# A wait of POOL for p, filler products at set-up and seam, late statistics moved behind the seam, W a on DVE

## The chip, the core and the metric

The kernel runs on one core of a Trainium2 chip. The core has a matrix engine (PE), a vector engine (DVE), an activation engine (ACT), a general engine (POOL) and a queue that issues transfers (SP); each works through its own instructions in order and waits on semaphores for the others. The metric is the device time in microseconds from start to end of one execution; the median of three runs is given.

## The reference

There are 128 graphs of 128 nodes with 256 features. Two residual layers follow each other:

```
n  = layernorm(x);  Wh = n @ W
e  = leaky(Wh@a1 [i] + Wh@a2 [j], 0.2) + log(adj + 1e-6)
x1 = x + softmax_j(e) @ Wh
m  = layernorm(x1)
w  = softmax(mean_graphs(m) @ Wr + br)              # per node, 8 experts
h  = relu(bn1(m @ W1[e] + b1));  h = relu(bn2(h @ W2[e] + b2))
out = x1 + sum_e w[node, e] * (h @ Wo[e] + bo[e])
```

So the gate w of a node needs the normalised x1 of all graphs, and no output can be formed before the last graph has gone through the first layer.

## The kernel before, in words

Four graphs are a group; there are G = 32 groups. The program has two blocks with a barrier between them, here called the seam: the graph stage and the expert stage.

**Graph stage.** Every engine runs `step(g, layer)` for g = -1 to 33, software-pipelined by hand: in step g, PE projects group g, scores and p are formed for a = g - 1, the product with p and x1 for b = g - 2, and the sum of normalised x1 over graphs (`acc`, in the tile resb) for h = g - 4. x1 of even groups lies in the tile h2, x1 of odd groups in w_bc. Steps 6 to 21 are a loop of 8 pairs (layer = 1, here the first loop), in which W1's seven Strassen combinations are prepared, one expert a pair; steps 22 to 29 are a loop of 4 pairs (layer = 2, the second loop) which splits W2 into a high and a low part, one expert a step.

DVE in a step: accumulator adds for two graphs (`add_part`, L608), l_sb (leaky scores, L621), the reciprocal, neg_m (L628), x1 (L646), four p with row sums (L658), statistics of the next x (`stats_1`, L574) and of x1 (`stats_2`, L582). POOL in a step: in the first loop four small sums into w_stage (even step, L451 to L458) or wq_lo (odd step, L463); in the second loop w_lo (L468); then the accumulator add of the other two graphs (L476); then `deviations` (L404 to L424), which turns statistics into dev, the reciprocal standard deviations, for the next x and for an x1. ACT in a step: s_sb (L506), the scaled x1 for POOL (L514), the high parts of weights, e_sb (L526), wh scaled by dev (L541), copies of pT (L557) and xnT (L562). PE in a step: the product p h (L733), the projection (L716), transposes of p (L753), of the next x (L685) and of the scores' column (L762). SP loads x, res and adj, stores x1, and in the first loop waits for wq_lo ahead of the next W1.

At set-up W is centred (its column mean, by a product with the constant tile mean_w, L694, is taken off, L587), then transposed, and W a1 and W a2 are formed on PE and copied into two further columns of the tile gw by way of ACT (L701 to L708, L493 to L496). Then the first projection starts. In the last steps DVE normalises the first tile for the experts (`tile_normalise`, L124) and splits it (`tile_low`, L162), and POOL forms its Strassen sums (`tile_sums`).

**Expert stage.** A unit is one expert of one tile of four graphs; a step handles the first layer of unit n (Strassen products, `strassen`, L1155), the second layer of unit n - 1 (`product`, L171) and the third of unit n - 3 (L1174). DVE's z for the second half of a unit (`sum_2`, L1042) has to be there before the last first-layer product of that unit. At its start DVE takes the statistics of the last group (L1029 to L1033), POOL their deviations (L918 to L925), and DVE adds group 30 to acc (`add_group`, L179); `feature_mean` in step 1 adds group 31 and forms the mean. POOL also forms the low parts of Wo there (L929). SP stores each tile's output when its last half is done (L905).

What orders the work around the change is written out by hand; there is no planner.

## Time and profile before

| | us |
|---|---|
| median of three runs | 2380.46 |
| lowest, highest | 2379.27, 2383.46 |
| the profiled execution | 2380.82 |
| its span, first to last instruction | 2379.0 |

| engine | busy us of the span | share |
|---|---|---|
| PE | 2339.6 | 98% |
| DVE | 1687.8 | 71% |
| ACT | 1615.7 | 68% |
| POOL | 435.0 | 18% |

The shares are means over both stages. The mean granted clock of PE over the span is 0.994; it has two levels, 1.2 and 2.4 GHz, and 1.00 is the upper one. A row of a window is its start and end, its length, each engine's busy time with its number of instructions, the clock, the share in which the DMA engines were busy, and their rate. A line such as L658 is line 658 of the kernel; a helper's line stands for all its callers. In a timeline, `x4` merges four instructions, and what stands in brackets is the idle time of the engine just before and what ended it.

### The profile page before, as it was taken

To read this page: it belongs to the slowest core of one execution; us is meant where nothing else is said; L and a number is where in the kernel's file an instruction comes from. 1 tells how busy PE (TensorE), PEld (TensorE's weight loads), DVE (VectorE), ACT (ScalarE), POOL (GpSimd) and SP (SyncE) were. 2 spreads that over 40 slices of the span, in tenths; PEclk is the share of its full clock that TensorE was granted. 3 is DMA by queue.
4 is the path that set the end of the run, shared out by engine and by line. 5 is a ranking of instruction groups with operands and counts; after the bars stand their busy time and mean duration, and the time that the engine had idled before them with its cause. 6 is when DMAs were issued, how large, how long until landed. Compare 5 with 4: busy or idle time off the path is not lost.

```text
span 2379.0 us, 46022 instructions
## 1 busy us (share of the span) xinstructions
PE 2339.6 (98%) x16164; PEld 2166.8 (91%) x16164; DVE 1687.8 (71%) x2577; ACT 1615.7 (68%) x2524; POOL 435.0 (18%) x566
## 2 busy tenths in 40 slices
PE   8999799999999999999999999999999999999999
PEld 7777689999999999999999999999999999999998
DVE  5999866666776766676666676666666666677666
ACT  5888676666666666666666666666666666666665
POOL 4898621111101011111111101011111111001010
PEclk9999799999999999999999999999999999999999
DMA  5778410000000000000000000000000000000000
GB/s 175 255 251 267 154 36 27 27 26 26 26 26 25 19 9 26 26 26 26 26 26 26 26 26 18 20 14 26 26 26 26 26 26 26 26 26 18 18 10 27
DMA packets 91178, 116.16 MB, mean 49 GB/s; under 512 B 4700, under 2 KB 78856, under 8 KB 91144
## 3 DMA queue, kind: packets, MB, share of 16 engines
q1 hardware_dynamic: 91144, 115.73, 14.8%
q8 instruction: 19, 0.31, 0.1%
q14 instruction: 15, 0.12, 0.0%
HBM read 82.16 MB, written 33.55 MB: 49 GB/s over the span
## 4 chain that ended last, share of the span: by engine, by line
PE 88%; DVE 0%; ACT 0%; issue 0%
PE ps_y L1174 31%; PE ps_wide L171 30%; PE ps_wide L1155 26%; PE ps_t L132 1%; DVE h_lo L1059 0%; DVE z L1052 0%; ACT h_hi L954 0%; ACT v L959 0%; DVE resb L1082 0%; DVE h_lo L1065 0%; DVE z L1042 0%; PE ps_t L1219 0%; PE ps_t L1201 0%; PE ps_t L1206 0%; ACT featT L985 0%
## 5 line engine op out<-in xcount | busy, mean ns | idle before, releaser
L959 ACT ACTIVATE v<-ps_wide,bn_cols 128x256 f32<-128x256 f32 x768 | 434.1, 565 | 375.0 <-PE ps_wide L1155 245.1
L967 ACT ACTIVATE h<-ps_wide,bn_cols 128x512 f32<-128x512 f32 x512 | 399.2, 780 | 314.2 <-PE ps_wide L171 312.0
L1174 PE MATMUL ps_y<-wo_hi,h_hi 128*128 128x256 f32 x2048 | 579.3, 283 | 0.5 <-DVE h_lo L1065 0.5
L1174 PE MATMUL ps_y<-wo_lo,h_hi 128*128 128x256 f32 x2048 | 579.6, 283 | 0.0
L1174 PE MATMUL ps_y<-wo_hi,h_lo 128*128 128x256 f32 x2048 | 579.5, 283 | 0.0
L1059 DVE SCALAR_TENSOR_TENSOR h_lo<-z,h_hi 128x1024 fp32r<-128x1024 f32 x256 | 313.8, 1226 | 341.6 <-ACT h_hi L954 341.6
L1155 PE MATMUL ps_wide<-xq_hi,wq_hi 128*128 128x256 f32 x1792 | 500.9, 279 | 7.4 <-PEq L185 3.1
L1155 PE MATMUL ps_wide<-xq_lo,wq_hi 128*128 128x256 f32 x1792 | 497.8, 278 | 0.0
L1155 PE MATMUL ps_wide<-xq_hi,wq_lo 128*128 128x256 f32 x1792 | 497.0, 277 | 0.0
L171 PE MATMUL ps_wide<-h_hi,w_lo 128*128 128x512 f32 x1024 | 403.9, 394 | 0.0
L171 PE MATMUL ps_wide<-h_lo,w_hi 128*128 128x512 f32 x1024 | 402.0, 393 | 0.0
L171 PE MATMUL ps_wide<-h_hi,w_hi 128*128 128x512 f32 x1024 | 398.3, 389 | 0.5 <-DVE h_lo L1059 0.5
L1174 PEld LDWEIGHTS ps_y<-wo_hi,h_lo 128*128 128x128 f32 x2048 | 392.5, 192 | 0.0
L1174 PEld LDWEIGHTS ps_y<-wo_hi,h_hi 128*128 128x128 f32 x2048 | 390.4, 191 | 1.1 <-DVE h_lo L1065 0.7
L1174 PEld LDWEIGHTS ps_y<-wo_lo,h_hi 128*128 128x128 f32 x2048 | 390.6, 191 | 0.0
L1065 DVE TENSOR_TENSOR h_lo<-h,h_hi 128x1024 fp32r<-128x1024 f32 x256 | 313.5, 1225 | 85.3 <-ACT h_hi L973 82.1
L938 POOL TENSOR_TENSOR resb<-resb,w_bc 128x512 f32<-128x512 f32 x64 | 85.4, 1336 | 1543.4 <-DMA resb<-x_scratch 1537.4
L1155 PEld LDWEIGHTS ps_wide<-xq_hi,wq_hi 128*128 128x128 f32 x1792 | 340.1, 190 | 19.0 <-issue 3.8
L1155 PEld LDWEIGHTS ps_wide<-xq_hi,wq_lo 128*128 128x128 f32 x1792 | 338.4, 189 | 9.8
L1155 PEld LDWEIGHTS ps_wide<-xq_lo,wq_hi 128*128 128x128 f32 x1792 | 338.2, 189 | 0.0
L1082 DVE SCALAR_TENSOR_TENSOR resb<-ps_y,w_node,resb 128x512 f32<-128x512 f32 x448 | 333.3, 744 | 3.9 <-PE ps_y L1174 3.9
L1052 DVE SCALAR_TENSOR_TENSOR z<-ps_wide,bn_cols,v 128x512 f32<-128x512 f32 x256 | 191.9, 750 | 153.4 <-PE ps_wide L1155 145.9
(131 smaller groups left out, 2995.6 us busy)
## 6 DMA issues: line engine op xcount, KB each, us to landing
x_sb<-in_x SPq DMA_DIRECT2D x32, 512.0 KB, 4.0
res<-in_x SPq DMA_DIRECT2D x32, 512.0 KB, 5.9
x1t<-x_scratch SPq DMA_DIRECT2D x32, 512.0 KB, 3.2
resb<-x_scratch SPq DMA_DIRECT2D x32, 512.0 KB, 3.2
out<-resb SPq DMA_DIRECT2D x32, 512.0 KB, 2.9
adj_sb<-in_adj SPq DMA_DIRECT2D x32, 256.0 KB, 6.1
x_scratch<-h SPq DMA_DIRECT2D x16, 512.0 KB, 4.7
x_scratch<-w_bc SPq DMA_DIRECT2D x16, 512.0 KB, 4.9
```

The lines of the kernel that those rows point to most:

```text
L132: last = nc.tensor.transpose(ps_x[:, c, b4 * N:(b4 + 1) * N], x1t[:, b4, c * P:(c + 1) * P], ident[:, :])
L171: mm = nc.tensor.matmul(acc_ps, w[:, i, c, cols], s[:, c, :], start=start and n == 0, stop=stop and n == len(terms) - 1)
L938: nc.gpsimd.tensor_tensor(resb[:, g, :], resb[:, g, :], ysum[:, g, :], ALU.add).then_inc(resb_done, 1)
L959: nc.scalar.activation(v[:, slot, :], ps_l1[:, 0, 0:H], ACT.Identity, bias=bn_cols[:, 1, cols], scale=bn_cols[:, 0, cols]).then_inc(done, 1)
L967: nc.scalar.activation(h2[:, m, :], ps_l2[:, m, :], ACT.Relu, bias=bn_cols[:, 3, cols], scale=bn_cols[:, 2, cols]).then_inc(r2_done, 1)
L1052: nc.vector.scalar_tensor_tensor(out=z[:, 0, :], in0=ps_l1[:, 1, :], scalar=bn_cols[:, 0, C * e:C * e + 1], in1=v[:, 0:2, :].rearrange("p ...
L1059: nc.vector.scalar_tensor_tensor(out=h1_lo[:, :, :], in0=z[:, :, :], scalar=0.0, in1=h1_hi[:, :, :].bitcast(F32), op0=ALU.max, op1=ALU.sub ...
L1065: nc.vector.tensor_tensor(h2_lo[u[1] % 2][:, :, :], h2[:, :, :], h2_hi[u[1] % 2][:, :, :].bitcast(F32), ALU.subtract).then_inc(lo2_done, 1)
L1082: nc.vector.scalar_tensor_tensor(out=dst[:, g, :], in0=ps_y[:, g, :], scalar=w_node[:, e:e + 1], in1=old, op0=ALU.mult, op1=ALU.add).then_ ...
L1155: mm = nc.tensor.matmul(out_ps, w[:, e, q, :], x[:, q, :], start=start and n == 0, stop=stop and n == len(terms) - 1, skip_group_check=True)
L1174: mm = nc.tensor.matmul(ps_y[:, b4, :], h[:, c, cols], w[:, e, c, :], start=(k == 0 and b4 % per_bank == 0), stop=(k == len(terms) - 1 and ...
```

## The change

- POOL waits in every step of the graph stage for both halves of p of group g - 1 before its first op.
- The statistics of group 0 are taken ahead of the steps; those of x1 of groups 30 and 31 behind the seam, for both together, with their deviations on POOL; both `add_group` calls now stand in `feature_mean`, and ACT waits for the first of them ahead of its first write to h2.
- At set-up a is loaded broadcast to all partitions, DVE forms W a1 and W a2 as four products with row sums ahead of the centring, and PE and a small DVE op centre the two columns. The transposes, ACT copies and small products are gone.
- PE runs filler products whose results nobody reads: seven on mean_w at set-up, five and four in the last two steps of the graph stage, six in each of units 0, 1 and 2 and twelve in unit 0.
- An Exp on ACT stands ahead of everything else of ACT.
- `tile_normalise` of the first tile stands behind p instead of ahead of x1; the third `tile_low` behind the last x1.
- The last tile's output is stored in two halves.

```diff
 # POOL, graph stage
                 def step(g, layer):
+                    a = ago(g, 1)
+                    if exists(a):
+                        pool.wait_ge(p_done, 2 * num(a) + 2)
                     if layer == 1 and g[1] == 0:
...
-                    if exists(nxt) or is_step(g, G - 1) or is_step(g, G):
+                    if exists(nxt) or is_step(g, G - 1):
                         deviations(nxt)
 # ACT, graph stage
+                act.wait_ge(mean_w_set, 1)
+                nc.scalar.activation(neg_m[:, :], mean_w[:, 0:GB], ACT.Exp)
 # DVE, graph stage
+                for b4 in range(GB):
+                    stats_1((0, 0), b4)
+                dve.wait_ge(proj_loaded, 2 * 16)
+                for c in range(C):
+                    for k in range(2):
+                        last = nc.vector.scalar_tensor_tensor(
+                            out=x1t[:, 2 * c + k, :], in0=gw[:, c, 0:D], scalar=1.0, in1=a_bc[:, k, :], op0=ALU.mult,
+                            op1=ALU.mult, accum_out=gw[:, c, D + k:D + k + 1])
+                last.then_inc(va_ready, 1)
...
+                dve.wait_ge(va_mean_ready, 1)
+                nc.vector.scalar_tensor_tensor(out=gw[:, :, D:D + 2], in0=gw[:, :, D:D + 2], scalar=2.0,
+                                               in1=ps_wide[:, 1:2, 0:2].to_broadcast([P, C, 2]), op0=ALU.mult,
...
-                    with_stats = exists(b) and not is_step(b, G - 1)
+                    with_stats = exists(b) and not is_step(b, G - 2) and not is_step(b, G - 1)
...
                     if is_step(g, G):
-                        for group in range(3):
-                            tile_low(dve, 0, group)
+                        tile_low(dve, 0, 0)
+                        tile_low(dve, 0, 1)
+                    if is_step(g, G + 1):
+                        tile_low(dve, 0, 2)
 # PE, graph stage
+                pe.wait_ge(mean_w_set, 1)
+                for _ in range(7):
+                    nc.tensor.matmul(ps_wide[:, 3, 0:P], mean_w[:, :], mean_w[:, :], start=True, stop=True)
                 pe.wait_ge(setup_done, 1)
                 next_rows((0, 0))
...
+                pe.wait_ge(va_ready, 1)
                 for c in range(C):
+                    last = nc.tensor.matmul(ps_wide[:, 1, 0:2], mean_w[:, :], gw[:, c, D:D + 2], start=(c == 0),
+                                            stop=(c == C - 1))
+                last.then_inc(va_mean_ready, 1)
+
+                def keep_clock(n):
+
+                    for _ in range(n):
+                        nc.tensor.matmul(ps_wide[:, 0, 0:D], ident[:, :], gw[:, 0, 0:D], start=True, stop=True)
...
+                    if is_step(g, G + 1):
+                        keep_clock(4)
...
+                    if is_step(g, G):
+                        pe.wait_ge(wh_copied, G)
+                        keep_clock(5)
 # expert stage: SP, POOL, ACT, DVE, PE
+                    if isinstance(t, int) and t == G - 1:
+                        sp.wait_ge(y_done, 2 * E * G - 1)
+                        sp.dma_start(out_g[t, :, 0:HB, :], resb[:, 0:HB, :]).then_inc(out_stored, 16)
+                        sp.wait_ge(y_done, 2 * E * G)
+                        sp.dma_start(out_g[t, :, HB:GB, :], resb[:, HB:GB, :]).then_inc(out_stored, 16)
...
+                pool.wait_ge(last_bnst, 1)
+                nc.gpsimd.tensor_tensor(last_dif[:, :, :], last_st[:, :, :, 1], last_st[:, :, :, 4],
+                                        ALU.subtract).then_inc(last_step, 1)
...
+                        if starts(prev, 0):
+                            act.wait_ge(acc_done, 1)
                         relu_2(prev, 0)
...
-                for b4 in range(GB):
-                    last = nc.vector.bn_stats(last_st[:, b4, :], x1[(G - 1) % 2][:, b4, :])
+                for i in range(2):
+                    for b4 in range(GB):
+                        last = nc.vector.bn_stats(last_st[:, i, b4, :], x1[(G - 2 + i) % 2][:, b4, :])
                 last.then_inc(last_bnst, 1)
...
-                add_group(G - 2)
...
                 def feature_mean():
+                    dve.wait_ge(last_rstd_done, 1)
+                    add_group(G - 2)
                     dve.wait_ge(acc_done, 1)
-                    dve.wait_ge(last_rstd_done, 1)
                     add_group(G - 1)
...
+                def keep_clock(n):
+
+                    for _ in range(n):
+                        nc.tensor.matmul(ps_y[:, 0, :], wq_hi[:, 0, 0, :], xq_hi[:, 0, :], start=True, stop=True)
...
+                    if starts(new, 0) or starts(new, 1) or starts(new, 2):
+                        keep_clock(6)
                     if exists_unit(new):
                         pe.wait_ge(v2_done, uno(new) + 1)
...
+                    if starts(new, 0):
+                        keep_clock(12)
                     if exists_unit(new):
                         pe.wait_ge(z2_done, uno(new) + 1)
```

## Rows read from the trace of the kernel before

**Rows 1.** Windows by stage: PE, PEld, DVE, ACT, POOL busy, clock, DMA, GB/s.

```profile
63.00:188.00 125.00, 118.85 (x642) 99.24 (x641) 122.63 (x402) 106.34 (x280) 112.18 (x185) 1.00 0.77 251
188.00:252.00 64.00, 59.02 (x321) 49.85 (x321) 61.71 (x201) 53.66 (x144) 50.62 (x78) 1.00 0.85 276
...
280.30:297.50 17.20, 14.20 (x51) 12.18 (x52) 11.37 (x25) 7.07 (x12) 4.93 (x7) 0.53 0.35 113
297.50:2376.00 2078.50, 2075.05 (x14799) 1946.30 (x14797) 1428.64 (x1752) 1395.19 (x1948) 215.20 (x194) 1.00 0.07 24
2376.00:2379.00 3.00, 0.00 (x0) 0.00 (x0) 0.00 (x0) 0.00 (x0) 0.00 (x0) 0.94 0.51 175
```

**Rows 2.** Timeline of DVE (start us, us, engine line op): neg_m, one a group.

```profile
62.98 0.69 DVE L628 TENSOR_REDUCE neg_m<-l_sb 128x4 f32<-128x512 f32 x1
...
187.88 0.69 DVE L628 TENSOR_REDUCE neg_m<-l_sb 128x4 f32<-128x512 f32 x1
...
251.89 0.69 DVE L628 TENSOR_REDUCE neg_m<-l_sb 128x4 f32<-128x512 f32 x1
...
269.11 0.69 DVE L628 TENSOR_REDUCE neg_m<-l_sb 128x4 f32<-128x512 f32 x1
```

**Rows 3.** Timeline, first loop, an even step.

```profile
127.81 0.54 DVE L658 SCALAR_TENSOR_TENSOR p_sb<-adj_sb,e_sb 128x128 f32<-128x128 f32 x1
...
131.58 0.85 DVE L608 SCALAR_TENSOR_TENSOR resb<-w_bc,dev,resb 128x256 f32<-128x256 f32 x2
```

**Rows 4.** Timeline, first loop, the odd step ahead of it.

```profile
118.72 1.65 POOL L424 TENSOR_TENSOR dev<-ve,minus_half 128x8 f32 x1 [0.19 <-POOL ve L420]
...
119.84 0.29 DVE L658 SCALAR_TENSOR_TENSOR p_sb<-adj_sb,e_sb 128x128 f32<-128x128 f32 x1
...
120.33 2.17 POOL L463 TENSOR_TENSOR wq_lo<-w_stage,wq_hi 128x896 f32 x1
...
122.47 1.26 POOL L476 TENSOR_TENSOR resb<-resb,x1s_high 128x512 f32<-128x512 f32 x1
...
123.10 1.31 DVE L608 SCALAR_TENSOR_TENSOR resb<-h,dev,resb 128x256 f32<-128x256 f32 x2
...
124.70 0.69 DVE L621 SCALAR_TENSOR_TENSOR l_sb<-s_sb 128x512 f32<-128x512 f32 x1 [0.29 <-ACT s_sb L506]
```

**Rows 5.** Timelines of POOL and DVE, second loop.

```profile
214.13 1.29 POOL L468 TENSOR_TENSOR w_lo<-w_stage,w_hi 128x512 f32 x1 [0.70 <-ACT w_hi L532]
...
214.22 1.35 DVE L658 SCALAR_TENSOR_TENSOR p_sb<-adj_sb,e_sb 128x128 f32<-128x128 f32 x1
```

**Rows 6.** Timeline, set-up, and one projection of the first loop.

```profile
8.05 0.69 DVE L587 SCALAR_TENSOR_TENSOR gw<-gw,ps_wide 128x512 f32<-128x512 f32 x1 [8.05 <-PE ps_wide L694]
...
12.99 5.52 PE L716 MATMUL ps_wide<-gw,xnT 128*128 128x258 f32 x16 [0.26 <-ACT gw L496]
...
124.94 3.65 PE L716 MATMUL ps_wide<-gw,xnT 128*128 128x258 f32 x16
```

**Rows 7.** Timelines of PE, DVE and POOL around the seam.

```profile
271.95 0.77 PE L753 MATMUL ps_pT<-ident,p_sb 128*128 128x128 f32 x4 [2.82 <-DVE p_sb L658]
...
273.47 2.89 DVE L162 TENSOR_TENSOR xq_lo<-xs,xq_hi 128x256 fp32r<-128x256 f32 x3
...
278.72 1.26 POOL L476 TENSOR_TENSOR resb<-resb,x1s_high 128x512 f32<-128x512 f32 x1
...
280.35 1.41 DVE L1029 BATCH_NORM_STATS2 last_st<-w_bc 128x6 f32<-128x256 f32 x4 [1.35 <-PEq L185]
```

**Rows 8.** Timelines, first units of the expert stage.

```profile
280.90 0.41 PE L1155 MATMUL ps_wide<-xq_lo,wq_hi 128*128 128x256 f32 x1
...
286.93 2.50 POOL L929 TENSOR_TENSOR wo_lo<-w_stage,wo_hi 128x512 fp32r<-128x512 f32 x2 [2.19 <-ACT wo_hi L1021]
...
291.56 1.67 DVE L179 SCALAR_TENSOR_TENSOR resb<-w_bc,dev,resb 128x256 f32<-128x256 f32 x4
...
297.51 0.28 PE L1155 MATMUL ps_wide<-xq_hi,wq_hi 128*128 128x256 f32 x1
```

More of the change, by code:

```diff
@@ L75, in adj_ffn @@
         bn_cols = sb("bn_cols", [P, 4, EC])
-        last_st = sb("last_st", [P, GB, 6])
-        last_mv = sb("last_mv", [P, GB, 2])
+        last_st = sb("last_st", [P, 2, GB, 6])
         mean_all = sb("mean_all", [P, G, GB])
@@ L327, in _ @@
                 sp.dma_start(gw[:, :, 0:D], gnn_w.rearrange("(c p) n -> p c n", p=P)).then_inc(proj_loaded, 16)
-                sp.dma_start(a_rows[:, :], gnn_a.rearrange("(r p) o -> r (p o)", p=P)).then_inc(proj_loaded, 16)
+                sp.dma_start(a_bc[:, :, :].rearrange("p k n -> p (k n)"),
+                             gnn_a.rearrange("n o -> (n o)").partition_broadcast(P)).then_inc(proj_loaded, 16)
                 load_x((0, 1))
@@ L489, in _ @@
             def _(act):
+                act.wait_ge(mean_w_set, 1)
+                nc.scalar.activation(neg_m[:, :], mean_w[:, 0:GB], ACT.Exp)
                 act.wait_ge(xnT_ready, C)
                 nc.scalar.activation(xnT[:, :, :], ps_xT, ACT.Copy).then_inc(xnT_copied, C)
-                act.wait_ge(proj_T, 1)
-                nc.scalar.activation(gwT[:, :, :], ps_wide[:, 1:1 + C, 0:D], ACT.Copy)
-                nc.scalar.activation(a_cols[:, :], ps_s[:, 0, 0:2 * C], ACT.Copy).then_inc(proj_T_copied, 1)
-                act.wait_ge(va_ready, 1)
-                nc.scalar.activation(gw[:, :, D:D + 2], ps_s[:, 1, 0:2 * C].rearrange("p (c k) -> p c k", k=2),
-                                     ACT.Copy).then_inc(va_copied, 1)
                 def step(g, layer):
@@ L629, in step @@
                                                 negate=True).then_inc(neg_m_done, 1)
-                    if is_step(g, G - 2):
-                        dve.wait_ge(dev_done, 4)
-                        tile_normalise(dve, 0, range(HB))
-                        tile_normalise(dve, 0, range(HB, GB))
                     if exists(b):
@@ L662, in step @@
                                 last.then_inc(p_done, 1)
-                    if exists(nxt):
+                    if is_step(g, G - 2):
+                        dve.wait_ge(dev_done, 4)
+                        tile_normalise(dve, 0, range(HB))
+                        tile_normalise(dve, 0, range(HB, GB))
+                    if exists(nxt) and not is_step(nxt, 0):
                         wait(dve, dev_done, num(nxt) - 1)
@@ L696, in _ @@
                 last.then_inc(col_mean_ready, 1)
-                pe.wait_ge(gw_centred, 1)
-                for m in range(C):
-                    for c in range(C):
-                        nc.tensor.transpose(ps_wide[:, 1 + m, c * P:(c + 1) * P], gw[:, c, m * P:(m + 1) * P], ident[:, :])
-                nc.tensor.transpose(ps_s[:, 0, 0:2 * C], a_rows[:, :], ident[0:2 * C, 0:2 * C]).then_inc(proj_T, 1)
-                pe.wait_ge(proj_T_copied, 1)
-                a_pair = a_cols[:, :].rearrange("p (k m) -> p m k", k=2)
-                for c in range(C):
-                    for m in range(C):
-                        last = nc.tensor.matmul(ps_s[:, 1, 2 * c:2 * c + 2], gwT[:, m, c * P:(c + 1) * P],
-                                                a_pair[:, m, :], start=(m == 0), stop=(m == C - 1))
-                last.then_inc(va_ready, 1)
+                pe.wait_ge(va_ready, 1)
+                for c in range(C):
+                    last = nc.tensor.matmul(ps_wide[:, 1, 0:2], mean_w[:, :], gw[:, c, D:D + 2], start=(c == 0),
[4 more added lines that the diff above has]
+                        nc.tensor.matmul(ps_wide[:, 0, 0:D], ident[:, :], gw[:, 0, 0:D], start=True, stop=True)
                 def project(g, graphs):
@@ L780, in psb @@
                 return sbk.enter_context(nc.psum_tensor(name, shape, F32))
-            last_ve = sbb("last_ve", [P, GB])
+            last_dif = sbb("last_dif", [P, 2, GB])
+            last_sum = sbb("last_sum", [P, 2, GB])
+            last_means = sbb("last_means", [P, 2, GB])
+            last_sqr = sbb("last_sqr", [P, 2, GB])
+            last_ve = sbb("last_ve", [P, 2, GB])
+            last_var = sbb("last_var", [P, 2, GB])
             mean_rstd = sbb("mean_rstd", [P, G, GB])
@@ L815, in adj_ffn @@
             w3_done = semb("w3_done")
+            last_step = semb("last_step")
             last_ve_done = semb("last_ve_done")
@@ L903, in body @@
                         load_x1(sp, t + 2)
-                    sp.wait_ge(y_done, 2 * E * (t + 1))
-                    sp.dma_start(out_g[t], resb[:, :, :]).then_inc(out_stored, 16)
+                    if isinstance(t, int) and t == G - 1:
[3 more added lines that the diff above has]
+                        sp.dma_start(out_g[t, :, HB:GB, :], resb[:, HB:GB, :]).then_inc(out_stored, 16)
+                    else:
+                        sp.wait_ge(y_done, 2 * E * (t + 1))
+                        sp.dma_start(out_g[t], resb[:, :, :]).then_inc(out_stored, 16)
                 body(0, False)
@@ L1027, in _ @@
             def _(dve):
-                for b4 in range(GB):
-                    last = nc.vector.bn_stats(last_st[:, b4, :], x1[(G - 1) % 2][:, b4, :])
+                for i in range(2):
+                    for b4 in range(GB):
+                        last = nc.vector.bn_stats(last_st[:, i, b4, :], x1[(G - 2 + i) % 2][:, b4, :])
                 last.then_inc(last_bnst, 1)
-                dve.wait_ge(last_bnst, 1)
-                for b4 in range(GB):
-                    last = nc.vector.bn_aggr(last_mv[:, b4, :], last_st[:, b4, :])
-                last.then_inc(last_stats_done, 1)
-                add_group(G - 2)
                 def sum_2(u):
```

40 lines of the change are left out of this document (22 added, 18 removed).

## The prediction

> **What bounds the kernel now.** I read the table of windows first, one row a stage [rows 1]. The program is two stages. In the graph stage (0 to 280 us) DVE has the most to do: 122.63 of 125.00 us in its first loop, 61.71 of 64.00 in its second. In the expert stage PE is busy 2075.05 of 2078.50 us, at the full clock; nothing of the change touches its loop, so those 2078 us stay. The change can only act on the 300 us ahead of it and on the last three. In the 17 us after the seam the mean granted clock is 0.53: PE runs at 1.2 GHz nearly all of it. Next I read the starts of neg_m, one a graph group [rows 2]: a pair of groups takes (187.88 - 62.98)/8 = 15.61 us in the first loop and (251.89 - 187.88)/4 = 16.00 in the second. Last, the timeline in order of time of single steps [rows 3 to 8].
>
> **How DVE and POOL meet.** A large POOL op holds up a DVE op that reads two SBUF tensors. In the first loop's even step the second p waits for the w_stage sums (0.54 us against 0.29) [rows 3, 4]; in the odd step the pair of accumulator adds waits for POOL's L476 (1.31 against 0.85: 0.46 lost to the 0.63 us that L476 still ran) [rows 3, 4]; in the second loop one p waits 1.35 - 0.29 = 1.06 us for w_lo [rows 5]. The small 1.65 us power of dev holds nobody up: p beside it takes 0.29 [rows 4]. The Trainium skill (SBUF - State Buffer, "SBUF: two separate sides") says otherwise, that the shared pair is held for the whole instruction and the loser fully blocks. By it the new set-up products would wait out the power of the first group, and the sum below would be 1 us longer; I go by the row.
>
> **Set-up: -4.5 (-6 to -2.5).** Centring W ends at 8.74, the first projection starts at 12.99 [rows 6]: 4.25 us for transposes, ACT copies, small products and a copy. All go. In their place come the first statistics, moved ahead (1.4 us by the like-sized L1029 [rows 7]; they need only x, and W is later, so they hide), and four DVE products 128x256 with an accumulator. No such row stands; the two-tensor add of that size takes 0.43 [rows 3] and is the lower end, twice that the upper; I take 0.47 each, near the add, since p with its accumulator is no dearer a column. That is 1.9. They start when a has landed: the mean products, over at 8.05 [rows 6], had W by 7 at the latest, and a's broadcast, 256 KB at some 250 GB/s [rows 1], adds up to 1; I take 6.4 (bounds 5.9 and 8). Then centring, 0.69, from 8.3 to 9.0, beside it PE's two small mean products, a second tiny centring, 0.2, and semaphores: the projection at 9.5, 3.5 earlier. The broadcast sits ahead of x's second tile in SP's queue and delays it by up to 1 us; it is not needed before 9. The Exp pulled forward on ACT moves the table load off the first copy; that copy isn't last any more, so nothing. The seven matmuls on mean_w fill PE until x lands and may delay its transposes by 0.3. They may lift the clock early: the first projection took 5.52 us, a steady one 3.65 [rows 6], so up to 1.9. But PE idles again between 7.5 and 9.5; I take half, -1.0. Next in line would be the batch-norm rows' loads, which PE needs only after the projection.
>
> **POOL's wait for p, first loop: +3.3 (-1 to +5).** Counted from the second p of a step: the add starts 3.26 later (119.84 to 123.10) [rows 4], takes 0.85 unhindered, and the next second p comes 127.81 - 124.41 = 3.40 behind, 0.29 of it waited for s_sb [rows 3, 4]: 7.2 us without a stall. POOL now starts only behind the fourth p, at 0.43 + 0.29 + some 0.15 = 0.88, and its large work takes 3.40 (120.33 to 123.73) [rows 4]: it ends at 4.28. The add, wanting to start at 3.26, finds L476 running with 1.02 to go; by the 0.46 lost for 0.63 it loses about 0.85. A step takes 8.0, a pair 16.0 against 15.61; times 8 is +3.1, and +0.2 for dev being later for ACT's wh. The p stalls are gone and the same lock is paid at the add, in both steps of the pair. Queued behind the waiting POOL: sums, wq_lo, L476, then the deviations that ACT's wh needs; SP's queue waits for wq_lo before all its other loads, 0.4 us later than now.
>
> **Second loop: -4.2 (-6.4 to -2).** Here the large work is w_lo and L476, 2.58 us (1.29 of w_lo [rows 5], and L476's as in [rows 4]); started at 0.88 it ends at 3.46, just behind the add's 3.26: 0.05 lost. DVE alone would allow 14.4 a pair; DVE's idle there (64.00 - 61.71 = 0.6 a pair [rows 1]) is ACT's s_sb, and this chain (deviations, wh, s_sb) grows into the bound: I take 14.95, so -1.05 times 4.
>
> **First and last groups: -2.5 (-3.5 to 0).** The steps ahead of the first loop have one p stall of L476's size, about 1.1, and two steps at the end the like (252 to 270): the stalls go, some 0.8 of 3.3 comes back as waits for s_sb. Moving tile_normalise behind p changes the order on a full DVE: p is earlier, the sum the same.
>
> **End of the graph stage: -2.4 (-3 to -1.2).** Blocks end with a barrier; POOL's last L476 ends at 279.98, and DVE starts again at 280.35 [rows 7]. Without the last deviations POOL runs L476 as soon as ACT has scaled x1, and ends near 276.7. DVE becomes last: it drops 1.4 of statistics [rows 7], its three tile_low (2.89 [rows 7]) run with less of POOL beside them, the third behind the last x1. It ends near 277.6. The fillers (five and four matmuls, 0.46 each, by the projection's 3.65 for 8) lie in PE's waits of 2.82 us before 271.95 and of 3 before the seam [rows 7]. If they keep the clock up, the last h products take half as long (on x1's path, counted here).
>
> **Behind the seam: +1.7 (-3 to +3.5).** Let the stage start at 0. DVE's h_lo of unit 0 ended as L179 starts, at 291.56 - 280.35 = 11.2 [rows 7, 8]; the 24 products ahead of it gain some 0.1 each at the full clock (0.28 against 0.41 [rows 8], spacing alike): 9.0. Unit 0's second layer, 12 products, ends near 11.8; before, it ended at 297.51 - 280.35 = 17.2 [rows 7, 8]. But the last product of unit 1 needs DVE's z, which stands behind feature_mean. That begins at 9.0 and now holds both add_groups, 1.67 each [rows 8] (the first stood in a free place: DVE idled ahead of unit 0's z), and 2.5 of sums: 5.8. POOL is busy with wo_lo then (2.50 for two [rows 8]; later than before, for it first works on the statistics: small ops and a 1.65 power [rows 4], from 2.8 to 6.8): one of them, 1.2, falls between the add_groups. z with its 0.7 is done at 16.7, against 17.2: -0.6. And PE idles from 11.8 to 16.6 with no filler there. The clock fell after PE's idle 2.82 at the seam [rows 7] and was low behind it [rows 1], so I expect it to fall here, and the uneven unit 2 that follows to run at 1.2 GHz: 5 us of products at double length, partly in waits, +2.3. ACT's new wait for the first add_group costs nothing while l2 of unit 0 comes at the same 10.7.
>
> **Last store: -0.8 (-1.3 to 0).** DMA was busy 0.51 of the last 3.00 us [rows 1]: 1.53 for 512 KB; half of it now goes ahead.
>
> **Sum.** -4.5 + 3.3 - 4.2 - 2.5 - 2.4 + 1.7 - 0.8 = -9.4. The profiled execution took 2380.82 us (span 2379.0), so 2371.4; the median of the three runs is 0.4 below it: **2371.0**.
>
> **Rivals.**
> 1. The lock spares it (12): L476 slips in ahead of the add, the first loop costs nothing, and the clock holds behind the seam. -9.4 - 3.3 - 2.3 = -15: 2365.4. For it: the odd step lost only 0.46 so far. Against: 1.02 us of overlap, more than the 0.63 that cost 0.46.
> 2. No change: the POOL wait costs more (18): L476 misses its turn, is held behind add and l_sb, dev and s_sb follow late: first loop 16.5 a pair (+4 more), second 15.5 (+2.2). -3.2: 2377. For it: L476 starts only some 0.2 ahead of the add when the sums run long.
> 3. Slower (8): the clock falls in the graph loop. PE waits longer per step (8.0 us for 7 of work, in one piece at the add's stall). If it falls once a pair, a projection takes up to 5.5 instead of 3.65 and PE becomes the bound: 8 times 1.85 = +14.8, -9.4 + 14.8 = +5.4: 2386. It decides from six falls on. Against: 63 to 252 us have clock 1.00 [rows 1] although PE waits there too.
>
> Forecast as above: 62. A measurement here tells 0.2%, 4.8 us, from no change. Faster: 62 + 12 = 74; within 0.2%: 18, rival 2; slower: 8. The range reaches from rival 1's time less 2 for the set-up's bound to rival 2's plus 2: 2363.5 to 2379.
>
> **What would show it.** Neg_m pairs near 16.0 in the first loop and 15 in the second; p never over 0.35 us; the add at 1.7 for two; the projection's start at 9.5; the second stage's first product at 270 or so (280.34 less set-up 4.5, loops 3.4 and seam 2.4); an idle of 4 to 5 us on PE ahead of unit 1's last product with the clock at half behind it; unit 3 onwards as before. Wrong it would be if the add isn't held, if s_sb bounds both loops, or if the expert loop itself moves.

## The result, and the profile of the changed kernel

The kernel before took 2379.94 us (median of 4 runs of that comparison), the changed kernel 2409.89 (2407.3 to 2410.68, 4 runs): a ratio of 1.0121, 95% interval 1.0103 to 1.0138. It is 30 us slower where 9 us faster was forecast, outside the range. The profiled execution took 2407.3 us, its span 2405.5. Windows by stage of the changed kernel (columns as in [rows 1]):

```profile
60.00:182.00 122.00, 116.19 (x622) 96.40 (x621) 122.00 (x386) 101.48 (x273) 107.09 (x180) 1.00 0.77 245
182.00:242.00 60.00, 57.57 (x319) 49.56 (x318) 57.99 (x200) 53.09 (x144) 49.57 (x81) 1.00 0.91 294
...
271.00:288.00 17.00, 12.62 (x72) 10.77 (x70) 11.56 (x22) 7.79 (x13) 8.55 (x13) 0.90 0.37 116
288.00:314.00 26.00, 25.51 (x160) 23.60 (x161) 14.02 (x23) 16.27 (x27) 8.58 (x6) 0.87 0.24 73
330.00:2380.00 2050.00, 2050.00 (x14387) 1912.68 (x14386) 1390.29 (x1704) 1355.82 (x1891) 203.03 (x182) 1.00 0.07 23
```

Up to the second stage all went roughly as forecast: its first product stands at 270.18 us, where the forecast had 270. PE's clock is 0.90 behind the seam, not the 0.53 of [rows 1]. The loss is in the last row, in the stage that the forecast left alone: PE is busy all the time, at the full clock, and does less. The same 650 us of both kernels, all products of PE counted (first before, then after):

```profile
400.00:1050.00 650.00, 650.00 (x4642) 610.11 (x4642) 448.35 (x551) 437.46 (x610) 65.82 (x60) 1.00 0.07 24
```

```profile
400.00:1050.00 650.00, 650.00 (x4568) 606.70 (x4568) 441.13 (x543) 430.59 (x601) 66.67 (x60) 1.00 0.07 24
```

4642 products against 4568: a product takes 1.6% longer, 33 us over the stage's 2078. Nothing waits: the products just start further apart. In the timeline of PE (start, duration), before has six products of layer 1 in 0.68 us, 0.113 each, and twelve of layer 3 in 1.44, 0.120 each:

```profile
1000.03 0.28 PE L1155 MATMUL ps_wide<-xq_hi,wq_hi 128*128 128x256 f32 x1
...
1000.71 0.28 PE L1155 MATMUL ps_wide<-xq_hi,wq_hi 128*128 128x256 f32 x1
...
1001.05 0.28 PE L1174 MATMUL ps_y<-wo_hi,h_hi 128*128 128x256 f32 x1
...
1002.49 0.28 PE L1155 MATMUL ps_wide<-xq_hi,wq_hi 128*128 128x256 f32 x1
```

After has

```profile
1001.74 0.28 PE L1189 MATMUL ps_wide<-xq_hi,wq_hi 128*128 128x256 f32 x1
...
1002.45 0.28 PE L1213 MATMUL ps_y<-wo_hi,h_hi 128*128 128x256 f32 x1
...
1003.17 0.28 PE L1213 MATMUL ps_y<-wo_hi,h_hi 128*128 128x256 f32 x1
```

that is six product starts from one row to the next: 0.118 for layer 1, 0.120 for layer 3. From 400 to 2200 us the mean from start to start is 0.1153, 0.1138 and 0.1137 us for layer 1's three terms before, 0.1204, 0.1194 and 0.1188 after (the stage has 5376 such products); layer 2's 0.2258 to 0.2316 became 0.2323 to 0.2338 (3072 products); layer 3 stayed within 0.002. A tile of four graphs, eight units, took 65.00 us and takes 66.09 in every tile: 32 times 1.09 is 35 us. Without it the change gives -5 or -6 us.

What can do that, with the same products on the same engine? Three theories. **A**: the tiles' places. The diff removes ones_cols ahead of wq_hi and doubles last_st, so by the order in which tiles are laid out (each rounded up to 32 bytes) wq_hi (layer 1's stationary operand) moves 32 bytes down a partition and xq_hi (its moving operand) 32 bytes up: xq_hi stands 64 bytes further from wq_hi. **B**: the fillers in PE's code shift how the loop's instructions are fetched. **C**: DVE, ACT or POOL run at another pace beside it.

### The profile page after: what moved, and what is told of

It reads as the page before. It is cut to its first block, busy times and chain, and to the rows that moved or that the text cites. A ratio compares the mean times of both kernels' runs of the same rounds, so it can differ in the third digit from the quotient of the medians.

```text
span 2405.5 us, 46160 instructions
## 1 busy us (share of the span) xinstructions
PE 2376.4 (99%) x16217; PEld 2192.5 (91%) x16217; DVE 1688.0 (70%) x2582; ACT 1611.6 (67%) x2522; POOL 428.9 (18%) x562
## 4 chain that ended last, share of the span: by engine, by line
PE 90%; DVE 5%; issue 2%; ACT 1%; POOL 1%; DVEq 0%; DMA 0%; SPq 0%; ACTq 0%; POOLq 0%
PE ps_y L1213 30%; PE ps_wide L168 30%; PE ps_wide L1189 26%; PE ps_wide L721 1%; PE ps_t L129 1%; DVE resb L613 1%; DVE st L573 1%; PE ps_th L738 1%; DVE h L647 1%; DVE st L565 1%; DVE w_bc L647 1%; DVE l_sb L626 1%; DVE p_sb L659 0%; POOL dev L417 0%; ACT xnT L553 0%
## 5 line engine op out<-in xcount | busy, mean ns | idle before, releaser
L1189 PE MATMUL ps_wide<-xq_hi,wq_hi 128*128 128x256 f32 x1792 | 509.8, 284 | 6.5 <-DVE z L1075 3.4
L1189 PE MATMUL ps_wide<-xq_hi,wq_lo 128*128 128x256 f32 x1792 | 506.0, 282 | 0.0
L1189 PE MATMUL ps_wide<-xq_lo,wq_hi 128*128 128x256 f32 x1792 | 505.8, 282 | 0.0
L168 PE MATMUL ps_wide<-h_hi,w_hi 128*128 128x512 f32 x1024 | 404.7, 395 | 0.6 <-DVE h_lo L1092 0.6
```

The lines of the kernel that those rows point to most:

```text
L168: mm = nc.tensor.matmul(acc_ps, w[:, i, c, cols], s[:, c, :], start=start and n == 0, stop=stop and n == len(terms) - 1)
L1189: mm = nc.tensor.matmul(out_ps, w[:, e, q, :], x[:, q, :], start=start and n == 0, stop=stop and n == len(terms) - 1, skip_group_check=True)
```

## The experiments

### Slid tiles

a_aligned is the kernel after with pads (unused tiles of 32 bytes); the others are the kernel before with pads. No instruction is added or removed in any.

```diff
 # a_aligned (on after), b_shifted (on before); also one pad at the head of each stage's own tiles
+        pad0 = sb("pad0", [P, 8])
         wq_hi = sb("wq_hi", [P, E, Q, P], F32R)
 # b_stationary (on before): pad0, and this one
+        pad3 = sb("pad3", [P, 8])
         w_stage = sb("w_stage", [P, Q + 1, P])
 # b_moving (on before): this one, and one at the head of each stage's own tiles
+        pad4 = sb("pad4", [P, 8])
         xq_hi = sb("xq_hi", [P, Q, H], F32R)
```

> The kernel after, with a tile of 32 bytes a partition put ahead of wq_hi (where ones_cols stood before), and one at the head of the graph stage's and of the expert stage's own tiles, so that every tile that TensorE reads in the expert loop starts again at a multiple of 64 bytes, as in the kernel before. No instruction is added or removed. Theory A (placement: the shared tiles slid by 32 bytes, and matmuls that read them became slower): the period of a tile goes from 66.10 back to 65.0 us, start to start of the first layer's products from 0.119 to 0.114 us, and the time is 2373 (2369 to 2377), about what the graph stage's gain alone gives. Theory B (PE's code: the filler products shift the loop's instructions and their fetch): nothing moves, 2408. Theory C (the pace of DVE, ACT or POOL in the loop): nothing moves, 2408.

> The kernel before, with the same 32-byte tile ahead of wq_hi, and one at the head of the graph stage's and of the expert stage's own tiles: all shared tiles now start at an odd multiple of 32 bytes, as in the kernel after; the stage's own stay at multiples of 64. Nothing else is changed. Theory A: the period goes from 65.0 to 66.1 us, the first layer's products from 0.114 to 0.119 us, the time to about 2415 (2408 to 2420). Theories B and C: no change, 2380.

> The kernel before, with only the four weight tiles wq_hi, wq_lo, w_hi, w_lo (TensorE's stationary operands of layers 1 and 2) slid by 32 bytes; all tiles behind them stand at multiples of 64 again. Theory A in the form that the stationary operand's place is what costs: nearly all of it here, layer 1 at 0.119 and layer 2 at 0.233 us, time about 2415. In the form that the moving operand is what costs: layer 1 stays at 0.114, and the time at 2380. Theories B and C: 2380.

> The kernel before, with only xq_hi and xq_lo (the moving operands of layer 1) slid by 32 bytes. Theory A, moving operand: layer 1 at 0.119, layer 2 unchanged at 0.229, time about 2409. Theory A, stationary operand: unchanged, 2380. Theories B and C: 2380.

| kernel | median us (runs) | ratio to before (95%) | us a tile | distance, bytes, layers 1 / 2 / 3 | layer 1, ns a product |
|---|---|---|---|---|---|
| before | 2380.24 (7) | | 65.00 | 64 / 64 / 0 | 114.3 |
| after | 2409.89 (4) | 1.0121 (1.0103 to 1.0138) | 66.09 | 128 / 32 / 0 | 119.5 |
| a_aligned | 2410.67 (4) | 1.0128 (1.0111 to 1.0145) | 66.11 | 128 / 64 / 0 | 119.5 |
| b_shifted | 2412.73 (4) | 1.0140 (1.0123 to 1.0157) | 65.99 | 64 / 96 / 0 | 118.2 |
| b_stationary | 2421.31 (4) | 1.0171 (1.0154 to 1.0188) | 66.30 | 96 / 96 / 0 | 119.5 |
| b_moving | 2410.67 (4) | 1.0129 (1.0112 to 1.0145) | 65.97 | 96 / 128 / 0 | 119.4 |

The distance is that of the moving operand from the stationary one, modulo 256 bytes, worked out from the order and sizes of the tiles; the last column is the mean over layer 1's three terms from 400 to 2200 us.

Three kernels with before's every instruction and only unused bytes added are 30 to 41 us slower. B can't do that, nor can C, unless the slide itself changed another engine's pace; places, below, has the effect with PE alone. But a_aligned stayed slow: the 64-byte form of A fell. It had before's rest modulo 64 everywhere, but not before's distance in layer 1. Nor do the three on before tell which operand of layer 1 counts: in each of them layer 2's distance changed as well (in b_moving the pad at the head of the stage's tiles moves h1, layer 2's moving operand). b_shifted kept layer 1's distance, and its layer 1 slowed all the same, to 118.2.

### Before's addresses, and what a place is

```diff
 # a_same (on after): pad0 as above; with pads in both stages, and the small tiles of the late statistics behind
 # wo_lo, every other tile that both kernels have lands on before's address
-        last_st = sb("last_st", [P, 2, GB, 6])
+        pad3 = sb("pad3", [P, 32])
...
             wo_lo = sbb("wo_lo", [P, E, C, D], F32R)
+            last_st = sbb("last_st", [P, 2, GB, 6])
 # b_all64 (on before)
+        pad0 = sb("pad0", [P, 16])
         wq_hi = sb("wq_hi", [P, E, Q, P], F32R)
 # b_wo64 (on before)
+            pad5 = sbb("pad5", [P, 16])
             wo_hi = sbb("wo_hi", [P, E, C, D], F32R)
 # places: PE alone; m and s the places of the operands in elements
+                for i in range(n):
+                    mm = nc.tensor.matmul(ps[:, i % 4, 0:cols], sta[:, s:s + P], mov[:, m:m + cols], start=True,
+                                          stop=True)
```

> The kernel after, with every tile that both kernels have at the very address of the kernel before (a 32-byte tile where ones_cols stood, 128 bytes where last_st and last_mv stood; the new last_st and the six small new tiles stand behind wo_lo). No instruction is added or removed. Theory A2 (placement, but by more than the rest modulo 64: both slid kernels of before were slow, and a_aligned had its tiles 64 bytes further than before from bn_cols on): the period of a tile is 65.0 us again and the time 2373 (2369 to 2378). Theory B (the filler products in PE's code) and theory C (pace of the other engines): 2409 still, which both slid kernels of before already speak against as the only cause; a mixed cause would give a time between.

> The kernel before, with every tile from wq_hi on slid by 64 bytes. All distances between the tiles stay, and so does the rest modulo 64. If only the distance of the two operands and the 64-byte rest matter: 2380, period 65.0. If the absolute place counts beyond 64 bytes (modulo 128 or more): between 2405 and 2420.

> The kernel before, with only wo_hi and wo_lo (moving operand of layer 3) slid by 64 bytes. In before, layer 3's operands have the same rest modulo 512 (128 and 128) and its 256-column products start every 0.120 us; layer 1's are 64 bytes apart (320 and 384) and start every 0.113 us. If a distance of 64 modulo 128 is what makes products fast: layer 3 goes to 0.113 to 0.115 us, 192 products a tile less 6 ns each, period 63.9 us, time about 2345 (2338 to 2360). If before's placement was luck of another kind: as the other slid kernels, 2405 to 2420.

> Computes nothing of the reference: it loads x, and TensorE runs groups of matmuls of type float32r from two large tiles, in 16 x 16 combinations of the place of the moving and the stationary operand, 0 to 480 bytes in steps of 32 (12 matmuls of 256 columns each), then 8 x 8 of 64-byte steps with 512 columns, then steps of 512 bytes to 16 KB; no other engine works beside it. Theory A2: start to start differs between the combinations, from 0.113 to 0.120 us at 256 columns, in a pattern by the two places. Rival (placement acts only through what DVE, ACT, POOL and DMAs do to the same memory at that time): all combinations alike within 1 ns.

a_same: 2373.89 us (11 runs), ratio 0.9969 (0.9956 to 0.9983), and 65.00 us a tile. That settles the cause: the changed kernel's 36 us over this one are the tiles' places alone. b_all64: 2380.51, ratio 0.9996 (0.9987 to 1.0005): sliding everything together costs nothing; distances count. b_wo64: 2390.61, ratio 1.0043 (1.0029 to 1.0057). The windows row of 650 us, a_same, then b_wo64:

```profile
400.00:1050.00 650.00, 650.00 (x4643) 610.10 (x4642) 448.28 (x551) 437.18 (x611) 65.44 (x60) 1.00 0.07 24
```

```profile
400.00:1050.00 650.00, 650.00 (x4613) 609.14 (x4612) 447.12 (x549) 435.44 (x607) 66.27 (x60) 1.00 0.07 24
```

In b_wo64 only layer 3's moving operand was slid. Layer 3 did become faster, 12 products in 1.41 us, but layer 1, whose tiles had not moved, went from 0.113 to 0.118, and the time fits neither forecast (2338 to 2360, or 2405 to 2420):

```profile
1000.88 0.28 PE L1156 MATMUL ps_wide<-xq_hi,wq_hi 128*128 128x256 f32 x1
...
1001.59 0.28 PE L1175 MATMUL ps_y<-wo_hi,h_hi 128*128 128x256 f32 x1
...
1003.00 0.28 PE L1156 MATMUL ps_wide<-xq_hi,wq_hi 128*128 128x256 f32 x1
```

places shows that a spacing depends on the distance and on something more. Nothing but PE works, and the spacing still differs (mean of start to start within a group, its first ones left out; at 256 columns 32 groups, at 512 columns 16, for each distance of the moving from the stationary operand modulo 256 bytes, whatever their absolute places):

| distance, bytes | 0 | 32 | 64 | 96 | 128 | 160 | 192 | 224 |
|---|---|---|---|---|---|---|---|---|
| ns, 256 columns, mean | 119.4 | 117.8 | 117.7 | 119.9 | 119.8 | 117.6 | 117.2 | 118.3 |
| lowest to highest | 119.2-120.0 | 116.6-118.1 | 117.6-117.9 | 119.6-120.2 | 119.1-120.0 | 117.0-120.0 | 113.4-117.9 | 118.2-118.4 |
| ns, 512 columns, mean | 227.5 | | 228.9 | | 231.1 | | 233.3 | |

Steps of 512 bytes and more changed nothing (117.8 to 117.9 in all 49). But one distance can have two spacings: at 192 bytes four groups ran at 113.4, each the first or second after the stationary operand's place had gone back to the start, and 28 at 117.7 to 117.9. The slid kernels agree with the table in layer 1: 119.4 or 119.5 at distances 96 and 128, 118.2 at 64 (b_shifted, b_wo64). The exception is the kernel before: at distance 64 most of its layer 1 products are 113 apart, where places has 117.7. So what ran ahead counts too; no short rule came out of this.

### The order of the products alone

> Computes nothing of the reference: TensorE alone runs the expert loop's order of products (57 a unit: 21 of layer 1, 12 of layer 2, 24 of layer 3, same shapes and strides) from small tiles, two units for each of 256 placements: xq, h1, h2 and wo slid by 0, 64, 128 or 192 bytes against wq and w; the first is before's placement modulo 256. Theory A2 (only the places of the operands modulo 256, and the order of products, set the spacing): before's placement gives 8.0 us a unit (its 65.0 less eight transposes, over 8), a_aligned's and b_wo64's give 8.16 and 8.07, and the best of the 256 lies below 8.0, perhaps 7.85. Rival (the other engines' traffic matters): before's placement differs from 8.0 by more than 0.05, and the order of the placements isn't that of the kernels.

Its 29412 products are the unit's 57 in order, for 256 placements of xq, h1, h2 and wo. Before's placement gave 8.007 us a unit, with no other engine at work; a tile of before is 8 of those and 0.94 us of transposes, 65.00. b_wo64's gave 8.060, so 65.42 a tile, where the kernel had 65.35. a_aligned's gave 8.197 (8.109 in the unit before: it had not settled), 66.5 a tile against 66.11. Most of the 256 lie above before's: the median of the 255 that could be read is 8.080, the highest 8.197, and 23 are below before's. **The kernel before had a lucky placement**: of the slides by multiples of 64 bytes nine in ten lose. The lowest is h2 slid by 64 bytes: 7.847. It was put into both kernels (s_h2_64 on a_same, b_h2_64 on before):

```diff
+            pad6 = sbb("pad6", [P, 16])
             h2_hi = [sbb(f"h2_hi{i}", [P, C, T], F32R) for i in range(2)]
...
+            pad7 = sbb("pad7", [P, 48])
             wo_hi = sbb("wo_hi", [P, E, C, D], F32R)
```

> a_same with only the four h2_hi and h2_lo tiles of the expert stage slid by 64 bytes (wo and what stands behind by 256, which the run of TensorE alone showed to be the same as none). Theory A2 (places modulo 256 and the order of the products set the spacing, whatever the other engines do): that run gives 7.847 us a unit here against 8.007 at before's placement, so a period of 65.0 - 8 x 0.16 = 63.7 us and 2373.9 - 32 x 1.28 = 2333 (2328 to 2345). Rival (the real kernel's placement acts in another way, or DVE or ACT become the bound at once): 2365 to 2410.

> The kernel before with the same slide of h2. Theory A2: 2380.2 - 41 = 2339 (2334 to 2351), period 63.7 us; the change's own worth against it is again the 6 to 7 us of the first 310 us. Rival: 2365 to 2410.

s_h2_64: **2342.29 us** (5 runs), ratio 0.9838 (0.9825 to 0.9851); b_h2_64: 2347.36, ratio 0.9858 (0.9843 to 0.9873). Both beat both kernels. The slide is worth 31.6 us on a_same and 33.0 on before; the rest of s_h2_64's 38 is the change's. A tile takes 64.00 us, not the 63.7 worked out. Timeline of s_h2_64, 12 products of layer 3 in 1.36 us, 0.113 each (their distance is now 192, where places had 113.4 too), and its 650 us:

```profile
1000.90 0.28 PE L1219 MATMUL ps_y<-wo_hi,h_hi 128*128 128x256 f32 x1
...
1002.26 0.28 PE L1195 MATMUL ps_wide<-xq_hi,wq_hi 128*128 128x256 f32 x1
```

```profile
400.00:1050.00 650.00, 650.00 (x4718) 608.59 (x4717) 456.24 (x560) 444.79 (x623) 65.17 (x60) 1.00 0.07 24
```

The missing 0.3 us a tile is seen too: behind the tile's eight transposes 28 products come every 118 ns before they go back to 113 with the same operands, and one product of layer 2 takes 333 ns to the next where its like take 226.

### The parts of the change, at before's addresses

```diff
 # s_nowait (a_same without it), b_wait (before with it)
+                    a = ago(g, 1)
+                    if exists(a):
+                        pool.wait_ge(p_done, 2 * num(a) + 2)
 # s_nofill (on a_same)
-                        keep_clock(4)
...
-                        keep_clock(5)
...
-                        keep_clock(6)
...
-                        keep_clock(12)
```

b_setup is before with the set-up's part of the diff, b_late before with the late statistics' part (last_bnst, feature_mean, tile_low, tile_normalise, ACT's wait).

> The kernel a_same (the kernel after with before's addresses) without POOL's wait for p; all the rest of the change stays. The prediction's terms for this wait: first loop +3.3, second loop -4.2, first and last groups some -2. So without it: first-loop pairs 15.6 instead of 15.7, second-loop pairs 16.0 to 16.1 instead of 15.0, w_lo and L476's like stall p again (p at 1.0 to 1.35 us in places), the accumulator adds faster; together 3 to 6 us slower than a_same, 2378 (2375 to 2381). Rival (the wait moves the stall from p to the adds and gives nothing): 2374.

> a_same without the filler products of the seam and the expert stage's start (five and four at the end of the graph stage, 6 + 6 + 6 + 12 in the first units); the seven at set-up stay. The prediction counts them at about -1 (the last h products and the 24 products ahead of the first h_lo at the full clock: 11.2 to 9.0 us) less what they cost where nothing waits. Theory 1 (the clock matters behind the seam): the granted clock falls before the seam and the first second-layer product comes 1.5 to 2.5 us later, time 2375.5 (2373 to 2378). Theory 2 (DVE's feature_mean and z set the start of unit 1's last product whatever PE does): equal, 2374, or 1 faster, because no filler stands in PE's way in units 1 and 2.

> The kernel before with only the set-up part of the change: W a from four DVE products and a broadcast of a, first statistics moved ahead of it, Exp table load pulled forward, seven filler products; every tile at before's address. The prediction's term is -4.5 (-6 to -2.5): first projection at 9.2 to 9.5 us instead of 12.99, all neg_m of both loops 4 to 5 us earlier, expert period 65.0; time 2376 (2374 to 2378). Rival (a part is given back at the seam, where other waits stand): 2378 to 2380.

> The kernel before with POOL's wait for p alone; before's addresses. The prediction's terms: first loop +3.3 (pairs 15.7 to 16.0 instead of 15.6), second loop -4.2 (pairs 15.0 instead of 16.1), first and last groups -1.5 of their -2.5: together -2.5, 2377.8 (2375 to 2380). Rival, from a_same against s_nowait (a gap of 6 us between the medians): 2374 to 2375. The phase of s_nowait's three long runs (odd steps of 10 us, POOL's wq_lo and L471 both lying on p) cannot come up here.

> The kernel before with the late statistics alone (statistics and add of the last two groups behind the seam, tile_low's third part one step later, tile_normalise behind p, ACT's wait for the first add); before's addresses. The prediction's terms: end of the graph stage -2.4 (of which some -0.5 for the fillers, not here), behind the seam +1.7: together about 0, 2380 (2377 to 2383), with the second stage's first product 1.5 to 2.5 us earlier and unit 1's last product no earlier than before, for z stands behind both adds in feature_mean. Rival (the fillers and the clock made that term, not the order of DVE): 2377 or less, with unit 2 on 3 us earlier.

| kernel | median us (runs) | ratio to before (95%) |
|---|---|---|
| s_nowait | 2380.07 (11) | 1.0013 (0.9994 to 1.0033) |
| s_nofill | 2373.89 (8) | 0.9974 (0.9963 to 0.9984) |
| b_setup | 2379.32 (12) | 0.9995 (0.9986 to 1.0004) |
| b_wait | 2374.81 (11) | 0.9977 (0.9968 to 0.9986) |
| b_late | 2380.26 (11) | 1.0000 (0.9991 to 1.0009) |

**The wait is what gains**: -5.6 us put into before, where the terms had -2.5 and the rival -5 to -6, and 6.2 lost when taken out of a_same. The fillers of the seam give nothing that can be told (2373.89 both ways), though they keep the clock up: over 252 to 270 us it is 1.00 in a_same and 0.81 in s_nofill. The late statistics alone give nothing either, as forecast. The set-up alone gave 0.9, not 4.5, with runs from 2374.87 to 2385.16; its interval reaches to -3.3. The three parts add up, within the noise, to the whole, -6.6, so the set-up's earlier start is nearly all lost again further on. Its profiled run, the longest, shows one place: one odd step of the first loop, where two p wait for wq_lo and POOL's add, and that pair of groups takes 18.8 us instead of 15.6. DVE, then POOL:

```profile
70.83 2.17 DVE L665 SCALAR_TENSOR_TENSOR p_sb<-adj_sb,e_sb 128x128 f32<-128x128 f32 x1
...
72.92 1.34 DVE L665 SCALAR_TENSOR_TENSOR p_sb<-adj_sb,e_sb 128x128 f32<-128x128 f32 x1
```

```profile
70.71 2.13 POOL L461 TENSOR_TENSOR wq_lo<-w_stage,wq_hi 128x896 f32 x1
72.81 1.30 POOL L474 TENSOR_TENSOR resb<-resb,x1s_high 128x512 f32<-128x512 f32 x1
```

In s_nowait that stall comes back. Three of its eleven runs took 2399.3 to 2400.1, the profiled one among them. There the first loop stayed in this other phase, with POOL's two large ops on p in every odd step (DVE, then POOL):

```profile
106.88 2.16 DVE L658 SCALAR_TENSOR_TENSOR p_sb<-adj_sb,e_sb 128x128 f32<-128x128 f32 x1
...
108.97 1.34 DVE L658 SCALAR_TENSOR_TENSOR p_sb<-adj_sb,e_sb 128x128 f32<-128x128 f32 x1
...
113.86 0.68 DVE L625 SCALAR_TENSOR_TENSOR l_sb<-s_sb 128x512 f32<-128x512 f32 x1
```

```profile
106.77 2.13 POOL L458 TENSOR_TENSOR wq_lo<-w_stage,wq_hi 128x896 f32 x1
108.85 1.31 POOL L471 TENSOR_TENSOR resb<-resb,x1s_high 128x512 f32<-128x512 f32 x1
```

Two p take 3.5 us instead of 0.6 and the step 10.1 (l_sb at 103.78, then 113.86); the odd steps behind it took 9.95 to 10.8 as well, to the end of the loop. None of the 30 runs with the wait and before's places (a_same, s_nofill, b_wait) took over 2377.1. One of before's runs, not profiled, took 2396.07; whether it was this phase isn't known. I had costed only the phase that the profile of before shows.

## Why the prediction was wrong, step by step

**"Nothing of the change touches its loop, so those 2078 us stay."** This step failed, and it alone put the result outside the range. I read the diff for instructions and not for the tiles that it adds and drops; it costs 36.0 us (2409.89 less 2373.89). The last sentence of the prediction names it as what would make it wrong, but no rival priced it. With before's addresses the change gives 2373.89, inside the range and 2.9 above the 2371.0. That this is close is partly luck: the first loop cost 2.5 less than its term, and the first and last groups, the end of the graph stage and the part behind the seam together came out 4.0 worse than theirs.

The other terms, by the timelines of after and a_same (the profiled a_same has a span of 2371.2, -7.8, where the sum had -9.4). Each is one profiled execution against one, and b_all64, which has before's instructions and time, tells how much of such a difference is chance: its loops are before's to 0.02 us, but its steps ahead of the first loop take 1.0 less, its last two steps 1.6 more, the end of the graph stage 0.8 less and the part behind the seam 2.9 more.

- **Set-up, -4.5: -4.9** (first neg_m, 23.92 to 19.01). The first projection starts at 9.15 us in after, 9.85 in a_same, forecast 9.5. The DVE products start when a has landed, at 6.76, and go every 0.35 us, not 0.47. POOL's power beside them did not hold them, as [rows 4] had it; the rule of the Trainium skill (SBUF - State Buffer, "SBUF: two separate sides"), by which the pair is held for the whole instruction, would have cost 1 us and did not show. The projection, at the full clock, took 3.75 us; the forecast had 5.52 less 1.0. Timelines of DVE, POOL and PE:

```profile
6.76 0.42 DVE L582 SCALAR_TENSOR_TENSOR x1t<-gw,a_bc 128x256 f32<-128x256 f32 x1 [0.98 <-DMA a_bc<-in_L_gnn_a]
...
7.11 0.42 DVE L582 SCALAR_TENSOR_TENSOR x1t<-gw,a_bc 128x256 f32<-128x256 f32 x1
...
7.80 0.42 DVE L582 SCALAR_TENSOR_TENSOR x1t<-gw,a_bc 128x256 f32<-128x256 f32 x1
```

```profile
7.33 1.10 POOL L417 TENSOR_TENSOR dev<-ve,minus_half 128x4 f32<-128x4 f32 x1
```

```profile
9.15 3.75 PE L721 MATMUL ps_wide<-gw,xnT 128*128 128x258 f32 x16 [0.25 <-DVE gw L592]
```

  That gain needs the clock. In b_setup the projection started as early, 9.92, but took 6.80 us at a mean clock of 0.85 over the first 23 us (1.00 in a_same), and the first neg_m came at 22.13, 1.8 and not 4.9 earlier than before's. Over all the profiles the first neg_m lies between 18.3 and 22.1 with the new set-up and between 22.3 and 25.1 with the old.

- **First loop, +3.3: +0.8.** Right mechanism, wrong size. p is never over 0.29 us and the lock is paid at the add, in both steps. The adds of two steps in after, and the L472 that each meets:

```profile
118.16 0.69 DVE L626 SCALAR_TENSOR_TENSOR l_sb<-s_sb 128x512 f32<-128x512 f32 x1
...
124.52 1.48 DVE L613 SCALAR_TENSOR_TENSOR resb<-w_bc,dev,resb 128x256 f32<-128x256 f32 x2
...
132.28 1.66 DVE L613 SCALAR_TENSOR_TENSOR resb<-h,dev,resb 128x256 f32<-128x256 f32 x2
133.86 0.69 DVE L626 SCALAR_TENSOR_TENSOR l_sb<-s_sb 128x512 f32<-128x512 f32 x1
```

```profile
124.05 1.27 POOL L472 TENSOR_TENSOR resb<-resb,x1s_high 128x512 f32<-128x512 f32 x1
...
131.99 1.27 POOL L472 TENSOR_TENSOR resb<-resb,x1s_high 128x512 f32<-128x512 f32 x1
```

  The pair, l_sb to l_sb, is 15.70, not 16.0. The price of the lock was right: where I had 0.85 lost for 1.02 us of overlap, the odd step's add loses 0.81 for 0.98 (132.28 to 133.26) and the even step's 0.63 for 0.80 (124.52 to 125.32), unhindered 0.85. The size that failed is the even step's work ahead of L472, four sums of w_stage, shorter than wq_lo: 0.22 a pair. The rest is the step without a stall, 7.13 us (7.76 less 0.63, 7.94 less 0.81) and not 7.2.
- **Second loop, -4.2: -3.7.** Pairs of 15.0, as forecast (four at 15.0 would be -4.0; the first step still had the first loop's 7.75).
- **First and last groups, -2.5: -0.7.** The steps ahead of the first loop gained 1.3, but the last two took 9.39 and 8.46 us in a_same against 9.28 and 7.93. In after l_sb of the last step stands 2.00 us idle. I had priced these steps by their stalls and not by who ends last in them. With b_all64's 1.6 in mind, this term isn't told from chance.
- **End of the graph stage, -2.4: -1.0** (last neg_m to the second stage's first product, 11.23 to 10.21). b_late has 10.07 without any filler, so the fillers gave none of it; b_all64 has 10.45 with nothing changed, so up to 0.8 of the 1.0 may be chance. DVE, not POOL, is last, as forecast, but its xq_lo parts are no faster than in [rows 7], 2.63 for two, and the adds there took 1.95:

```profile
262.91 2.63 DVE L159 TENSOR_TENSOR xq_lo<-xs,xq_hi 128x256 fp32r<-128x256 f32 x2
265.47 1.95 DVE L613 SCALAR_TENSOR_TENSOR resb<-w_bc,dev,resb 128x256 f32<-128x256 f32 x2
...
269.17 0.68 DVE L159 TENSOR_TENSOR xq_lo<-xs,xq_hi 128x512 fp32r<-128x512 f32 x1
```

- **Behind the seam, +1.7: +2.5** (first product to a full tile's add, 104.17 to 106.64). z of unit 1 stands behind both adds, as worked out:

```profile
281.27 1.66 DVE L176 SCALAR_TENSOR_TENSOR resb<-h,dev,resb 128x256 f32<-128x256 f32 x4
282.96 1.67 DVE L176 SCALAR_TENSOR_TENSOR resb<-w_bc,dev,resb 128x256 f32<-128x256 f32 x4
...
287.11 0.74 DVE L1075 SCALAR_TENSOR_TENSOR z<-ps_wide,bn_cols,v 128x512 f32<-128x512 f32 x1
```

  It ends 17.7 us after the stage's start, not 16.7, PE idles 3.4 us for it, and the clock falls there, as feared: 0.87 in the windows row of 288 to 314. b_late, without fillers, has +2.2. But how much of this the statistics cost isn't shown: b_all64, with before's instructions, takes 107.07 us from its first product to that add, 2.9 more than before. What differs is the clock: 0.53 in the first 17 us and then 1.00 in before, 0.70 and then 0.54 in b_all64. The 9 us from 17 us behind the first product on, before, then b_all64:

```profile
297.50:306.50 9.00, 7.53 (x48) 6.52 (x47) 5.08 (x9) 6.22 (x12) 2.44 (x2) 1.00 0.21 58
```

```profile
297.00:306.00 9.00, 7.58 (x28) 6.88 (x29) 5.20 (x9) 4.22 (x7) 0.56 (x1) 0.54 0.19 58
```

- **Last store, -0.8: -0.8** (7.0 at the last add, 7.8 at the span's end).

Of the rivals, 1 (first loop free) came nearest for the first loop: +0.8. 2 and 3 did not come up with the wait; without it, s_nowait's long runs lose 20 us, more than 3's 14.8, by another mechanism, a phase of POOL against p.

## What to carry to other kernels

Read a diff also for the tiles it adds, drops or resizes: with the engines' code unchanged, 32 unused bytes ahead of some of TensorE's operands cost 1.3 to 1.7%, and an experiment on a kernel whose products run back to back must keep its operands' distances, or it measures the placement. Where PE is busy all the time and slower per product at the full clock, look at start to start; a run of PE alone with the loop's order of products, over the placements modulo 256 bytes, found in one execution what was worth 32 to 33 us in the real kernel. A wait that makes two engines meet at a fixed place can be worth more than its mean gain: it also shuts out a worse phase. And compare two profiles term by term only after a third, of the old code, has told how far a term moves by itself.

## What the runs showed of the hardware

- The spacing of back-to-back float32r products depends on the distance of moving and stationary operand modulo 256 bytes and on what ran before: 113.3 to 120.2 ns for 256 columns (106.7 would be 256 at 2.4 GHz), with no other engine at work.
- The same operands can run at two spacings: layer 1 mostly at 113 ns through the whole stage in a_same and at 118 in b_wo64, and in s_h2_64 at 118 for 28 products behind the eight transposes of a tile and at 113 after them.
- Absolute places did not matter: 64 bytes for all tiles, 2380.51 against 2380.52 us; nor did steps of 512 bytes between the operands.
- POOL's power on 4 elements a partition (1.10 us) held none of the DVE products beside it (every 0.35 us), while a p beside wq_lo (2.13 us) took 2.17 us where its like take 0.28.
- Why it is 256 bytes, and what keeps a spacing, was not found out.
